# Key projection of two blocks in one 160-column product, and four strided key copies per block

## What is computed

```python
x = x + tanh(g_xattn[0]) * L0_xattn(layernorm(x), ctx)
x = x + tanh(g_ffn[0])   * L0_ffn(layernorm(x))      # mixture of 8 experts, top 2, and a shared one
x = x + tanh(g_xattn[1]) * L1_xattn(layernorm(x), ctx)
x = x + tanh(g_ffn[1])   * L1_ffn(layernorm(x))      # ternary weights
```

```python
q = (query @ Wq + bq).reshape(B, SQ, H, HD).transpose(0, 2, 1, 3)
k = (key_value @ Wk + bk).reshape(B, SK, H, HD).transpose(0, 2, 1, 3)
v = (key_value @ Wv + bv).reshape(B, SK, H, HD).transpose(0, 2, 1, 3)
scores = jnp.einsum('bhqd,bhkd->bhqk', q, k) * scale
```

## Time and profile before

| | |
|---|---|
| median of 3 runs | 1251.52 us (1249.58 to 1255.15) |
| the profiled execution | 1254.5 us, span 1252.8 us |
| mean granted TensorE clock | 0.977 |
| busy share of the span | PE 94%, PEld (weight loads) 88%, DVE 80%, ACT 63%, POOL 54% |
| instructions | 27020; PE 9168, DVE 2077, ACT 1521 |
| key copies `s_a_kd<-s_a_k_parts` | 252 from SP and 4 from ACT, 20 KB each |
| key product L782 | 256 records |

### The profile page before, as it was taken

One profiled execution on the slowest core, in us unless ns is written; L12 is line 12 of the kernel. 1 busy time (PEld: TensorE's weight loads), 2 busy tenths in 40 slices (PEclk: granted clock), 3 DMA queues, 4 the chain that ended last, 5 costly groups with the idle time before them and its releaser, 6 DMA issues.

```text
span 1252.8 us, 27020 instructions
## 1 busy us (share of the span) xinstructions
PE 1183.5 (94%) x9168; PEld 1107.2 (88%) x9169; DVE 999.3 (80%) x2077; ACT 786.0 (63%) x1521; POOL 678.8 (54%) x772
## 2 busy tenths in 40 slices
PE   6999999989888999999799999998999999899998
PEld 5999999979778999999689999998899998788887
DVE  5899999857797766666679999996987788888887
ACT  4777777758554555555367777775344445678774
POOL 5333443234104565563687777730465466788885
PEclk9999999979999999999879999998999999999999
DMA  3222221023201433334434333312100000000000
GB/s 102 55 56 62 64 52 52 20 67 120 67 1 40 117 106 106 100 110 102 117 62 75 61 65 65 63 25 82 38 2 0 0 0 1 1 26 25 26 26 34
DMA packets 72319, 68.67 MB, mean 55 GB/s; under 512 B 26624, under 2 KB 64256, under 8 KB 72000
## 3 DMA queue, kind: packets, MB, share of 16 engines
q1 hardware_dynamic: 57936, 47.78, 13.0%
q0 software_dynamic: 12576, 18.62, 8.2%
q10 hardware_dynamic: 1744, 1.50, 0.4%
HBM read 44.00 MB, written 18.61 MB: 50 GB/s over the span
## 4 chain that ended last, share of the span: by engine, by line
PE 75%; DVE 10%; ACT 5%; issue 4%; POOL 3%; DMA 1%; ACTq 0%; DVEq 0%; POOLq 0%; SPq 0%
PE PSUM L769 13%; PE PSUM L771 12%; PE PSUM L770 12%; PE PSUM L857 8%; PE PSUM L845 6%; PE PSUM L836 6%; PE PSUM L782 3%; PE PSUM L855 3%; POOL s_t_gh L2615 2%; PE PSUM L809 2%; PE PSUM L866 1%; PE PSUM L1915 1%; PE PSUM L2804 1%; PE PSUM L2805 1%; ACT s_m_xn L1412 1%
## 5 line engine op out<-in xcount | busy, mean ns | idle before, releaser
L2165 POOL TENSOR_TENSOR s_f_h_lo<-s_f_h,s_f_h_hi 128x512 fp32r<-128x512 f32 x64 | 93.6, 1468 | 104.3 <-ACT s_f_h_hi L2109 103.7
L1338 POOL DMA_INDIRECT s_m_tile_x<-normed_x,s_tokens x78 | 96.5, 1237 | 76.3 <-DVE s_tokens L1629 54.9
L857 PEld LDWEIGHTS PSUM<-s_a_v_diagonal,s_a_prob_t 128*128 128x128 f32 x1024 | 127.5, 194 | 0.0
L857 PE MATMUL PSUM<-s_a_v_diagonal,s_a_prob_t 128*128 128x36 f32 x1024 | 126.6, 270 | 0.0
L699 ACT ACTIVATE s_a_prob_t<-PSUM 128x640 f32<-128x640 f32 x128 | 90.1, 704 | 38.6 <-PE PSUM L845 37.8
L454 DVE TENSOR_REDUCE s_a_row_max<-PSUM 128x8 f32<-128x640 f32 x128 | 104.8, 819 | 9.0 <-PE PSUM L836 5.7
L461 DVE TENSOR_TENSOR s_a_less<-PSUM,s_a_row_max 128x640 f32<-128x640 f32 x128 | 105.0, 820 | 4.6 <-issue 0.2
L1006 POOL DMA_INDIRECT s_x<-sorted_y,s_slots x60 | 95.7, 1595 | 19.2 <-issue 13.6
L2103 ACT ACTIVATE s_f_h<-PSUM,s_cols 128x512 f32<-128x512 f32 x64 | 44.1, 689 | 89.4 <-PE PSUM L771 82.9
L845 PE MATMUL PSUM<-s_ident,s_a_prob 128*128 128x128 f32 x640 | 95.3, 281 | 0.5 <-ACT s_a_prob_t L699 0.2
L769 PE MATMUL PSUM<-s_m_x_hi,s_m_up_w 128*128 128x256 f32 x312 | 91.8, 294 | 1.1 <-issue 1.0
(11 more groups left out here) (327 smaller groups left out, 4243.8 us busy)
## 6 DMA issues: line engine op xcount, KB each, us to landing
sorted_y<-s_m_tile_y SPq DMA_DIRECT2D x39, 256.0 KB
s_a_kd<-s_a_k_parts SPq DMA_DIRECT2D x252, 20.0 KB
s_x<-x SPq DMA_DIRECT2D x16, 256.0 KB, 2.8
s_a_ctx<-ctx SPq DMA_DIRECT2D x32, 128.0 KB, 2.7
s_moe_raw<-moe_w SPq DMA_DIRECT2D x16, 256.0 KB, 3.4
normed_x<-s_m_xn SPq DMA_DIRECT2D x16, 256.0 KB, 3.3
y<-s_x SPq DMA_DIRECT2D x16, 256.0 KB, 2.1
s_late_raw<-moe_w SPq DMA_DIRECT2D x11, 256.0 KB, 2.8
```

The lines of the kernel that those rows point to most:

```text
L857: last = pe.matmul(a.o_ps[:, 2 * c:2 * c + 2, :], a.prob_t[j % 2][:, c, :], v[:, j // BT, 0, 2 * c:2 * c + 2], start=False, stop=c == PC - ...
L1338: pool.indirect_dma_start(m.tile_x[n % 2][:, t, :], None, d["normed_x"], bass.IndirectOffsetOnAxis(ap=tokens[:, BT * n + t:BT * n + t + 1] ...
L2165: pool.tensor_tensor(f.h_lo[m % 4][:], f.h[m % 4][:], f.h_hi[m % 4][:].bitcast(F32), ALU.subtract).then_inc(f.h_split, 1)
```

## The change

- The keys of two blocks (2p and 2p+1) are one product with 160 moving columns, from a context buffer that holds both. One half m of the outputs is made per turn: m = 0 in the even turn before the pair, m = 1 in the odd one. Turns 14 and 15 make none. The first pair of a stage is made whole ahead of the loop, in bank 5 (stage 0) or 6 (stage 1).
- ACT and DVE do one 160-column op per turn in place of two of 80.
- The columns of Wq and Wk and their biases are permuted on the host so that a head's 16 rows lie 4 apart, in both 64-row halves: one DMA of 32 strided rows takes a head of each half, so four per block. In an odd turn SP sends the next block's keys, waits for the last score of this turn's block, sends those of the block after, and loads the context of the pair after that. The first block of stage 0 has two copies from SP and two from ACT.
- PE and ACT write out three last turns, not one.

The diff, cut to its core:

```diff
+TILE_HEADS = HPC // 2
+KEY_STEPS = BATCH - 1
...
+    row = np.arange(P)
+    chunk_order = (row // (P // 2) * TILE_HEADS + row % TILE_HEADS) * HD + row % (P // 2) // TILE_HEADS
+    by_row = np.concatenate([m * P + chunk_order for m in range(KC)])
...
-                self.k_parts = [sb(scope, n + f"k_parts{z}", [P, 2, KC, CTXP], F32R) for z in two]
+                self.k_parts = sb(scope, n + "k_parts", [P, 2, 2, KC, CTXP], F32R)
...
-                self.ctx = [sb(scope, n + f"ctx{z}", [P, KC, P]) for z in two]
+                self.ctx_pair = sb(scope, n + "ctx", [P, 2, KC, P])
+                self.ctx = [self.ctx_pair[:, z] for z in two]
...
+                self.first_k_bank = PSUM[:, 5 + stage, :]
...
-        def spread_keys(engine, a, b, heads):
-            engine.wait_ge(a.k_split, b.count + 1)
+        def key_step(a, b):
+
+            return b.n + 2 + KEY_STEPS * a.stage
+
+        def send_keys(engine, a, b, heads):
             for h in heads:
-                rows = slice(h * HD, (h + 1) * HD)
-                engine.dma_start(a.kd[b.z][rows, :, :, h % (HPC // 2), :].bitcast(F32),
-                                 a.k_parts[b.z][rows].bitcast(F32)).then_inc(a.kd_in[b.z], 16)
+                engine.dma_start(a.kd[b.z][h::TILE_HEADS, :, :, h, :].bitcast(F32),
+                                 a.k_parts[h::TILE_HEADS, b.z].bitcast(F32)).then_inc(a.kd_in[b.z], 16)
...
+            def key_residue(m, bank):
+                return dve.scalar_tensor_tensor(a.k_parts[:, :, 1, m, :], bank.rearrange("p (z n) -> p z n", z=2),
+                                                cols[:, a.bk + m:a.bk + m + 1], a.k_parts[:, :, 0, m, :].bitcast(F32),
+                                                ALU.add, ALU.subtract)
...
             def keys(b):
-                dve.wait_ge(a.k_round, b.count + 1)
-                for m in range(KC):
...
+                dve.wait_ge(a.k_round, key_step(a, b))
+                key_residue(b.z, a.misc[:, 0:2 * CTXP]).then_inc(a.k_split, 1)
...
+                if ahead > 1:
+                    keys(b)
                 if ahead:
-                    keys(b.next())
                     value_tails(b.next())
...
+            def keys_rounded(b):
+                act.wait_ge(a.kv_ps, b.count + 2)
+                if b.z == 0:
+                    for z in range(2):
+                        act.wait_ge(a.kd_in[z], 16 * TILE_HEADS * (b.half + a.base // 2 + 1))
+                key_rounded(b.z, a.misc[:, 0:2 * CTXP]).then_inc(a.k_round, 1)
...
-            paired_blocks(act, BATCH, body, a.base)
+            paired_blocks(act, BATCH, body, a.base, 3)
...
+            def key_products(m, bank):
+                for k in range(KC):
+                    last = pe.matmul(bank.rearrange("p (z n) -> p z n", z=2),
+                                     a.w_raw[:, RAW_K, k * DIM + m * P:k * DIM + (m + 1) * P],
+                                     a.ctx_pair[:, :, k, 0:CTXP], start=k == 0, stop=k == KC - 1)
+                return last
+
+            def first_keys():
+                for z in range(2):
+                    pe.wait_ge(a.ctx_in[z], 16 * (a.base // 2 + 1))
+                for m in range(KC):
+                    last = key_products(m, a.first_k_bank[:, 2 * m * CTXP:2 * (m + 1) * CTXP])
+                return last
+
             def keys(b):
-                for m in range(KC):
...
+                if b.z == 0:
+                    for z in range(2):
+                        pe.wait_ge(a.ctx_in[z], 16 * (b.half + a.base // 2 + 2))
+                key_products(b.z, a.misc[:, 0:2 * CTXP])
...
+            def keys_values(b, ahead):
+                pe.wait_ge(a.x_split, b.count + 2)
+                if ahead > 1:
+                    keys(b)
+                pe.wait_ge(a.ctx_split, b.count + 2)
+                values(b.next())
...
-            paired_blocks(pe, BATCH, body, a.base)
+            paired_blocks(pe, BATCH, body, a.base, 3)
...
-                load_context(a, b)
 
             def load_context(a, b):
-                after(sp, a.kv_ps, b.count - 1)
...
+            def load_context_pair(a, b):
+
+                sp.wait_ge(a.ctx_split, b.count + 3)
+                load_context(a, b.next().next().next())
+                load_context(a, b.next().next().next().next())
+
+            def spread_first_pair(a):
+                first = Block(0, 0, 0, a.base)
+                spread_keys(sp, a, first, KEY_STEPS * a.stage + 1, range(TILE_HEADS if a.stage else TILE_HEADS // 2))
+                if a.stage == 0:
+                    sp.wait_ge(a.cleared, 3)
+                spread_keys(sp, a, first.next(), KEY_STEPS * a.stage + 1, range(TILE_HEADS))
+                sp.wait_ge(a.ctx_split, a.base + 2)
+                for b in (Block(2, 0, 1, a.base), Block(3, 1, 1, a.base)):
+                    load_context(a, b)
+
+            def spread_pair(a, b):
+
+                spread_keys(sp, a, b.next(), key_step(a, b), range(TILE_HEADS))
+                sp.wait_ge(a.scores_ps, UNITS * (b.count + 1))
+                send_keys(sp, a, b.next().next(), range(TILE_HEADS))
...
                 if ahead > 1:
                     load(a0, b.next().next())
                 if ahead:
                     load_moe(b.next())
-                    spread(a0, b.next())
+                if ahead > 1 and b.z:
+                    spread_pair(a0, b)
+                if ahead > 2 and b.z:
+                    load_context_pair(a0, b)
```

More of the change, by code:

```diff
@@ L528, in attention_on_vector @@
                 weight_residue(0)
-                keys(first)
+                first_keys()
                 weight_residue(1)
@@ L706, in attention_on_scalar @@
             first = Block(0, 0, 0, a.base)
-            keys_rounded(first)
+            first_keys_rounded()
             if a.stage:
-                values(first)
+                values(first, 0)
             x_rounded(first)
@@ L712, in attention_on_scalar @@
                 act.wait_ge(a.cleared, 2)
-                spread_keys(act, a, first, range(HPC // 2, HPC))
-                values(first)
+                spread_keys(act, a, first, 1, range(TILE_HEADS // 2, TILE_HEADS))
+                values(first, 0)
             act.wait_ge(a.mask_done, a.stage + 1)
@@ L730, in body @@
                 mask_laid(b, 2)
-                if ahead:
-                    keys_rounded(b.next())
+                if ahead > 1:
+                    keys_rounded(b)
                 exponential(b, 1)
@@ L735, in body @@
                 if ahead:
-                    values(b.next())
+                    values(b.next(), key_step(a, b) if ahead > 1 else 0)
                 transposed(b, 0)
@@ L790, in values @@
                          for k in range(KC)]).then_inc(a.kv_ps, 1)
-            def keys_values(b):
-                pe.wait_ge(a.ctx_split, b.count + 1)
-                if not (isinstance(b.n, int) and b.n == 0):
-                    pe.wait_ge(a.x_split, b.count + 1)
-                keys(b)
-                values(b)
+            def keys_values(b, ahead):
+                pe.wait_ge(a.x_split, b.count + 2)
+                if ahead > 1:
+                    keys(b)
+                pe.wait_ge(a.ctx_split, b.count + 2)
+                values(b.next())
             def transpose_x(b):
@@ L915, in attention_on_tensor @@
                 pe.wait_ge(mix.gated, SHARED + ALL)
-                keys_values(first)
+                first_keys()
+                pe.wait_ge(a.ctx_split, a.base + 1)
+                values(first)
                 last_of_mixture(ALL - 1)
@@ L939, in body @@
                 if ahead:
-                    keys_values(b.next())
+                    keys_values(b, ahead)
                 if behind:
@@ L2967, in _ @@
             sp.wait_ge(a1.cleared, 7)
-            spread(a1, Block(0, 0, 0, a1.base))
+            spread_first_pair(a1)
             def body(b, behind, ahead):
@@ L2974, in body @@
                     load_ffn(b.next())
-                    spread(a1, b.next())
+                if ahead > 1 and b.z:
+                    spread_pair(a1, b)
+                if ahead > 2 and b.z:
+                    load_context_pair(a1, b)
             paired_blocks(sp, BATCH, body, a1.base, 3)
```

62 lines of the change are left out of this document (30 added, 32 removed).

## The result

The changed kernel takes 1234.61 us (median of 6 runs, 1231.63 to 1236.64) beside 1253.34 for the kernel before on the same chip: ratio 0.986, 95% interval [0.984, 0.988]. One execution of the kernel before (3459.07 us) and one of experiment 10 (5871.93 us) stand far apart from all others and are left out of the ratios; without the first, the median before is 1251.52 us. So the change is faster: 1.4% of 1251.5 is 17 us. A second series of the same file gave 1236.31 and 0.988 [0.986, 0.990], 15 us. The forecast was 10.9 us less, 1240.6. The profiled execution took 1233.7 us (span 1232.0).

What follows compares the result with a forecast made beforehand. TensorE was taken to bound the attention loops (busy 14.55 of 14.6 us a turn). 8.3 + 1.6 + 1.2 - 0.2 = 10.9 us less gave 1240.6 us as a median; range 1235.5 to 1249.

Steps and rivals of the forecast that it cites:

- The key product: Steady turns: four 160-column records at 0.139 us replace eight of 0.111; 0.33 us less a turn, 8.3 in 25 turns.
- The rule of an isolated product: Key product: cost N/2.4 + 2.5 ns, columns alone, so merging saves TensorE nothing; as a rival 1251.5 us, chance 0.09.
- VectorE and ScalarE: Steady turns: merged residue and rounding take about 0.34 us each instead of 0.51 and 0.55, covering TensorE's shorter product.
- costed at nothing: Steady turns: VectorE's and ScalarE's shorter operations and VectorE's waits cover TensorE's 0.33 us gain, so none is lost.
- The rival's mechanism: Steady turns: VectorE sets the pace, so a turn gains only 0.17 us; 1245.0 us in all, chance 0.12.
- Turn 14s and what lies behind the loops: Turn 14 of each stage: no key product any more, 0.8 us less each, 1.6 in all.
- Turns at the lower clock: Three first turns at 1.2 GHz: product 0.62 us less each, 1.9 in all, counted as 1.2 (bounds 0 and 1.9).
- Copies and the Sync queue: Odd turns: eight copies at 0.63 us, then both context loads, hidden with 3 us to spare; late-queue rival 1268, chance 0.06.
- First product and start: the step that failed: Stage starts: doubled first product +0.43 us, in stage 0 covered; ScalarE's two fewer copies 1.5 us earlier; together +0.2.
- Of which 0.3 can show, as the query product ends no sooner: Stage 0 start: of the 1.5 us ScalarE gains by issuing two key copies instead of four, only 0.3 shows.
- the +0.2 and its bound of -0.5: Net cost of the doubled first product and moved copies at the start: +0.2 us, bounds -0.5 and +1.0.

Runs made afterwards that it cites:

- experiment 10: Kernel before, with ScalarE issuing two of the first block's eight key copies (Sync six) and the first key product of stage 0 made twice: 1253.14 us, ratio 1.000.
- Experiment 2: Changed kernel, with each half of the key outputs made by two products of 80 columns instead of one of 160: 1246.01 us, ratio 0.997 to the kernel before.
- 3: Changed kernel plus unused fp32 products of 40 to 320 columns in the last turn of stage 0, pricing a record by width: 1250.3 us in one execution.
- 12: Changed kernel plus unused products keeping TensorE busy ahead of its known waits in the first turns of both stages: 1239.73 us, ratio 0.991 to the kernel before.
- Experiment 6: Changed kernel, with each strided 32-row key copy cut into two of 16 rows, eight per block: 1266.76 us, ratio 1.012 to the kernel before.
- 8: Kernel before, with ScalarE issuing two of the first block's eight key copies in stage 0 and Sync six: 1250.80 us, ratio 1.000.
- 9: Kernel before, with the first key product of stage 0 made once more, unused: 1253.33 us, ratio 1.002.
- 11: Changed kernel, with all four key copies of stage 0's first block on Sync, none on ScalarE: 1235.09 us, ratio 0.986 to the kernel before.

## Why the prediction was right, and where it was off

**The key product.** Forecast 0.139 us a record and 0.33 a turn, 8.3 in 25 turns. Measured 0.135, and 0.355 in stage 0, 0.325 in stage 1: 4.26 + 3.58 for the 23 turns of B and F, so 8.5 for 25. Experiment 2 gives it back, 3 measures the price by width. The rule of an isolated product, the Trainium skill, page "TensorE: Matmul & The Clock Gate", section "Back-to-back issue gap", would have 40 columns at little over a quarter of 160; measured are 0.112 and 0.136, so for a stream of products with their own weights it doesn't hold here. What the same section says of such a stream, that load and product set the pace together, the trace agrees with: a flat part, and above it a price by columns.

**VectorE and ScalarE.** Forecast 0.34 us for the merged operation, measured 0.37 and 0.39, and "costed at nothing" held. Were the cover gone, it said, a turn would gain 0.17 to 0.27; with both operations split again a turn is still 0.25 shorter than before in stage 0 and 0.11 in stage 1. The rival's mechanism was real and 0.15 us away.

**Turn 14s and what lies behind the loops.** Forecast 1.6, and two products of turn 13 that C and G hold as well. From turn 13's product to the transposes of turn 14 in stage 1 (L866, now L908) it is 19.32 us before and 18.57 after: 0.75 less, where the forecast had 0.33 + 0.8. G as a whole gained 2.1 in the first profile of the changed kernel. The rest lies behind the transposes, where a part runs at 0.50: from those of turn 14 to the last ones it is 17.4 us in both profiles of the kernel before (841.90 to 859.35 in the first), 15.9 in the first of the changed one (822.61 to 838.55) and 17.0 in its second. At 0.50 stand 5.5 us of it in both of the former, 2.1 and 4.3 in the latter; less half of these it is 14.7 to 14.9 in all four. So this part comes and goes with the clock, and the forecast had no term for it.

**Turns at the lower clock.** Forecast 1.2 for three turns, at 0.62 each. The price was right: in turn 0 of stage 1 the product takes 616.65 - 615.62 = 1.03 us where it took 1.69.

```profile
615.62 1.44 PE L810 MATMUL PSUM<-s_a_ctx,s_a_w_raw 128*128 128x160 f32 x4 [1.41 <-DVE s_a_x_lo L429]
616.65 0.61 PE L798 MATMUL PSUM<-s_a_w_hi,s_a_ctx_hi 128*128 128x256 f32 x1
```

But nothing of it arrives: segment D is 37.74 and 38.86 us where it was 37.27 and 37.09. TensorE waits for VectorE ahead of the product, and behind that for GpSimd, as 12 shows.

**Copies and the Sync queue.** Forecast eight copies at 0.63, context loads 5.1 us behind the first copy, hidden. Measured 0.65, 5.45 behind, no wait on L810. Experiment 6 shows what the reserve was worth.

**First product and start: the step that failed.** "Of which 0.3 can show, as the query product ends no sooner", and with it the +0.2 and its bound of -0.5. The query product did end sooner: 13.92 + 0.28 - 6.56 = 7.6 us behind the first product's start, where it was 9.3. The doubled first product, costed only as work (+0.43), also filled TensorE's wait of 0.93 us ahead of the transposes, and the queries ran at the full clock; with two copies fewer on ScalarE the rounding could follow at once. Counted from VectorE's first normalised x, the first score came 1.0 us sooner in both profiles, with the copies alone (8) 0.45, near the forecast's 0.3, and with the product alone (9) no sooner. Turn 1's product came 1.8 and 2.5 us sooner behind the first product than in the better profile of the kernel before, 0.75 to 0.8 of which is the later start of that product, where the forecast had about 0.6 for turn 0.

The full clock itself comes early with the longer first product. Taken by the first row of the granted clock in a trace, where the pace of the records changes too, it begins at 9.9 to 12.2 us in all nine profiles whose first product makes both blocks, and at 15.3, 21.3 and 31.2 us in the three where it makes one. Made twice, it gives 10.7 (9) and 16.1 (10). So the one goes with the other, but not every time.

**What the parts add up to.** More profiles bear on the segments that their edits don't touch: 8, 9 and 10 on C to G of the kernel before, 11 on C, D, E and G of the changed one, 3 on all but C, 12 on G. Medians of these, and for the start and A the mean of two beside the median of three, give:

| part | forecast, us less | measured, us less |
|---|---|---|
| B and F, 23 steady turns | 7.6 | 7.8 |
| start, A, D and E | 1.0 | 2.9 |
| C and G | 2.3 | 4.0 |
| sum | 10.9 | 14.7 |

So the 15 to 17 us of the medians are nearly all there. The excess over the forecast is A, where the full clock comes early (33.4 before; 29.5, 30.3 and 31.0 after), and G, where 6.8 us stand at 0.50 in three of the five profiles with the changed code (13.7 and 17.0 in the others), and 10.2 or more in all five with the code of before.

**What is open.** Why G meets a little less of the lower clock, and whether it always does. The two profiles with the same mean clock of 0.981 (the second of before at 1245.3, the first of after at 1233.7) differ by only 11.6 us, near the forecast, but that is luck of the pair: the first is the fastest of all executions of the kernel before. That the changed kernel meets fewer stretches of the lower clock all over isn't borne out: the mean clock is 0.977 over the 58 executions of the kernel before that ran beside the experiments, and 0.978 over the 12 of the changed one, and at 0.978 five of the one take 1249.7 to 1254.4 us, five of the other 1235.0 to 1236.6. That mean leaves out what lies ahead of a trace's first clock row, so it says nothing of the start.

## What to carry to other kernels

For products that each load their own 128x128 weights, count records and not columns up to where the columns take longer (here some 133 columns of fp32); merging two 80-column products pays, merging four brings no more. When a step of the busiest engine is shortened, shorten its followers too and count the reserve of the engines close behind: here a third of a turn's gain hung on it in stage 0, and two thirds in stage 1. Cost a queue by its pieces, and name what stands behind them: halving the number of copies was not the gain, it was what let the rest of the change be free.

## What was not expected of the hardware

- The issue of a small copy costs the same for 16 rows (0.635 us) and 32 strided rows (0.65), while a context load of 128 rows takes 0.35 to 0.46.
- The granted clock reads 1.00 from 10.5 to 17.2 us in the first profile of before, while the records there run at half pace: 256 columns in 0.213 us, where they take 0.115 at the full clock. The trace has no clock row ahead of 31.2 us (15.3 in the second profile, 10.4 in the first of the changed kernel), and the column shows 1.00 where it has none. So the mean clocks of 0.977 and 0.981 are too high, the first by more, and at the start the pace of known records tells more than the column.
- Two executions of one kernel differ by 15 us (1233.7 and 1248.6), with the same time in the steady turns to 0.1 us; all of it lies outside them. A pair of profiles is compared there only after a second one of each. The steady turns aren't quite free of it either: with the first block's copies moved (8, 10), B of the kernel before took 175.0 us and not 175.6.
